# Moving the context projections of a five-stage decoder's fourth stage into its second stage, through DRAM

## The reference, cut to what matters

```
# second stage (first half): WKV over k = layernorm(x), v = ctx
y = wkv(w, u, k, v);  x = x + y
# fourth stage, per batch:
h  = layernorm(x)
q  = concat([ctx, h]) @ Wq                 # = ctx @ Wq[:256] + h @ Wq[256:]
k  = concat([h @ Wk,  ctx @ Wsk])          # 64 channels each
v  = concat([h @ Wv,  ctx @ Wsv])          # 64 channels each
x  = x + softmax(q k^T / sqrt(8) + alibi, windows 64 and 32) v @ Wo     # 32 query heads, 8 key heads
```

## Time and profile before

| | us |
|---|---|
| median of 3 runs | 808.35 |
| the runs | 806.6, 808.35, 809.21 |
| the profiled execution, as timed | 809.21 |
| its span, first to last instruction | 807.1 |

### The profile page before, as it was taken

One profiled execution on the slowest core, in us unless ns is written; L12 is line 12 of the kernel. 1 busy time (PEld: TensorE's weight loads), 2 busy tenths in 40 slices (PEclk: granted clock), 3 DMA queues, 4 the chain that ended last, 5 costly groups with the idle time before them and its releaser, 6 DMA issues.

```text
span 807.1 us, 19492 instructions
## 1 busy us (share of the span) xinstructions
PE 671.5 (83%) x6957; PEld 380.8 (47%) x6980; DVE 556.9 (69%) x1600; ACT 506.1 (63%) x1213; POOL 302.8 (38%) x488
## 2 busy tenths in 40 slices
PE   1789898854677589789999878999999999988985
PEld 0245555533445467444454444544455444544553
DVE  5478877688999994678787726455555555557776
ACT  3558888676677746388878743566555666565431
POOL 2214644295699958655565021112111211101110
PEclk9979999955689999899999999999999999999999
DMA  4757675200000001434535323322433234220001
GB/s 154 148 125 136 146 179 68 66 27 13 21 14 7 1 2 34 67 67 96 72 68 93 54 53 80 54 48 48 81 60 47 49 61 73 48 42 9 28 34 39
DMA packets 143104, 50.73 MB, mean 63 GB/s; under 512 B 131296, under 2 KB 140960, under 8 KB 142752
## 3 DMA queue, kind: packets, MB, share of 16 engines
q1 hardware_dynamic: 143008, 49.49, 31.1%
HBM read 15.64 MB, written 2.10 MB: 22 GB/s over the span
## 4 chain that ended last, share of the span: by engine, by line
PE 60%; DVE 13%; issue 9%; POOL 8%; ACT 6%; DMA 2%; SPq 1%; ACTq 0%; DVEq 0%; POOLq 0%
PE bank L1305 4%; PE bank L984 4%; PE bank L1255 3%; PE bank L946 3%; PE bank L1279 3%; PE bank L1237 2%; PE bank L959 2%; ACT l1x_probs L1199 2%; PE bank L995 2%; PE bank L1240 2%; PE bank L705 2%; PE bank L716 2%; PE bank L1331 2%; DVE l1a_neg_max L871 2%; PE bank L1005 2%
## 5 line engine op out<-in xcount | busy, mean ns | idle before, releaser
L1144 DVE TENSOR_REDUCE l1x_neg_max<-bank 128x2 f16<-128x448 f32 (+1 forms) x192 | 117.7, 636 | 98.9 <-PE bank L1262 98.9
L1199 ACT ACTIVATE l1x_probs<-bank 128x512 f32<-128x512 f32 x192 | 106.2, 596 | 41.9 <-PE bank L1283 24.9
L871 DVE TENSOR_REDUCE l1a_neg_max<-bank 128x4 f16<-128x512 f32 x128 | 83.3, 684 | 31.7 <-PE bank L959 31.0
L919 ACT ACTIVATE l1a_probs<-bank 128x512 f32<-128x512 f32 x128 | 69.7, 596 | 32.3 <-PE bank L973 31.2
L1097 POOL TENSOR_TENSOR l1x_rstd<-l1x_var_eps,minus_half 128x1 f32<-128x1 f32 x16 | 8.8, 548 | 203.4 <-DVE l1x_var_eps L1128 203.4
L1636 PE MATMUL bank<-mix_xT_parts,w_ternary 128*128 128x256 f16 x384 | 55.2, 302 | 14.4 <-DVE mix_hidden L1529 12.3
L558 DVE TENSOR_REDUCE l_neg_max<-bank 128x4 f16<-128x512 f32 x64 | 42.3, 684 | 17.4 <-PE bank L685 17.4
L1636 PEld LDWEIGHTS bank<-mix_xT_parts,w_ternary 128*128 128x128 f16 x384 | 39.5, 107 | 27.4 <-DVE mix_hidden L1529 11.4
L631 ACT ACTIVATE l_probs<-bank 128x512 f32<-128x512 f32 x64 | 36.8, 600 | 13.3 <-PE bank L705 13.3
L1460 POOL TENSOR_TENSOR mix_hidden_parts<-mix_hidden,mix_hidden_parts 128x256 f16<-128x256 f32 x48 | 35.8, 754 | 15.8 <-ACT mix_hidden_parts L1588 15.6
L1588 ACT CAST mix_hidden_parts<-mix_hidden 128x256 f16<-128x256 f32 x48 | 19.2, 403 | 31.2 <-DVE mix_hidden L1529 29.2
(11 more groups left out here) (268 smaller groups left out, 1877.3 us busy)
## 6 DMA issues: line engine op xcount, KB each, us to landing
x_residual<-x_in SPq DMA_DIRECT2D x4, 512.0 KB, 5.0
mix_ctx_in<-ctx_in SPq DMA_DIRECT2D x16, 128.0 KB, 2.0
l1x_ctx_in<-ctx_in SPq DMA_DIRECT2D x16, 128.0 KB, 2.1
out_dram<-moe_out SPq DMA_DIRECT2D x16, 128.0 KB, 1.7
w_f<-w_in SPq DMA_DIRECT2D x2, 704.0 KB, 6.3
w_attn_f<-w_l_in SPq DMA_DIRECT2D x1, 1024.0 KB, 6.8
q_stack<-q_begin_in SPq DMA_DIRECT2D x1, 1024.0 KB, 5.3
l1x_qT<-l1x_neg_maxT SPq DMA_DIRECT2D x64, 2.0 KB
```

The lines of the kernel that those rows point to most:

```text
L871: dve.tensor_reduce(mm[:, 16 * j + 4 * s:16 * j + 4 * s + 4], b_s[c % 3][:].rearrange("p (r k) -> p r k", k=P), AX.X, ALU.max, negate=True ...
L919: act.activation(prob[:, c, :], b_st[c % 2][:], ACT.Exp).then_inc(s_exp, 1)
L1144: dve.tensor_reduce(mm[:, first:first + count], scores, AX.X, ALU.max, negate=True).then_inc(s_max, 1)
L1199: act.activation(prob[:, c, :], b_st[c % 2][:], ACT.Exp).then_inc(s_exp, 1)
```

## The change

The second stage gets a piece `K` for each batch: PE multiplies the transposed context, which lies in SBUF as `vv`, by the 384 columns of `w_l1x_ctx`, into the batch's bank `b_kv[c]`; ACT copies the result to a buffer `cproj`; SP stores it to a new DRAM tensor `ctx_projected`. The bank is handed on only after that copy.

The fourth stage no longer loads or transposes the context. SP loads 320 of the 384 columns of a batch into `cp` (128 x 320), and brings the 64 V columns straight into the V tile `vs` with two DMAs of 64 rows each, in pieces of 8 numbers. `F7` is one projection of `x` with 384 columns. The high parts of the keys come from PSUM and from `cp`. The q of `x` and the q of the context are added by DVE (`F8`) into `pf`; ACT and POOL split `pf` into high and low parts. DVE makes the low part of the keys of `x` (`F8b`), POOL those of the context. V of `x` is copied by ACT in two instructions.

In the diff, the K pieces stand in the order SP, ACT, PE. The order tables of the second and the fourth stage are new on all engines, with their `PACE` entries, and those of the first and third stage keep their orders. PE's order in one turn of the fourth stage is now `ST.0 PV.1 S.3 ST.1 F5 S.4 T1.1 F7 ST.2 S.5 T4 ST.3 M T5 S.0 ST.4 PV.0 S.1 ST.5 T1.0 S.2`; SP's is `G X M V`. Two pairs of semaphores in the first stage are joined, scratch columns are kept apart, and two constants that place the FFN's weight preparation in the first stage move a little.

```diff
     ("mix", "sp"): order("""
-        W3.0+1 W3.1+1"""),
+        K.1-1 K.0 W3.0 W3.1"""),
     ("mix", "pe"): order("""
-        W3.1+1 HA.0-3 HA.1-3 G3-2 W11.0-1 HA.2-3 W3.0+2 W11.1-1 HA.3-3 HA.4-3 HA.5-3 D-4"""),
+        W3.1+1 K.0+1 W11.1-1 HA.3-3 G3-2 HA.4-3 HA.5-3 K.1+1 D-4 W3.0+2 HA.0-2 HA.1-2 HA.2-2 W11.0"""),
     ("l1x", "sp"): order("""
-        M-1 X+2 G+1"""),
+        G-2 X-1 M-3 V-3"""),
     ("l1x", "dve"): order("""
-        F1c+2 S.1 S.2 S.3 S.4 T1.0-2 F3+2 F1+3 S.5 S.6 T1b.0-2 T1.1-2 S.7 F1b+3 T1b.1-2 S.8 S.9 S.10 S.11 T5-2
-        S.0+1"""),
+        S.2 F1+3 S.3 S.4 F1b+3 T1.0-2 F3+2 S.5 S.6 T1b.0-2 S.7 S.8 T1.1-2 T1b.1-2 S.9 F8+2 S.10 S.11 F1c+3 T5-2
+        S.0+1 S.1+1 F8b+2"""),
     ("l1x", "act"): order("""
-        ST.0-1 V+1 ST.1-1 OE.1-2 F5+2 ST.2-1 ST.3-1 T4-2 ST.4-1 ST.5-1 F8a.0+2 F8a.1+2 ST.6-1 ST.7-1 M F8+2
-        OE.0-1 ST.8-1 ST.9-1 ST.10-1 ST.11-1"""),
+        ST.0-1 ST.1-1 V+1 OE.1-2 F5+2 ST.2-1 ST.3-1 F8a.0+2 ST.4-1 ST.5-1 T4-2 F8a.1+2 ST.6-1 M ST.7-1 ST.8-1
+        ST.9-1 OE.0-1 ST.10-1 ST.11-1"""),
     ("l1x", "pe"): order("""
-        PV.1-2 S.3 F5+2 ST.1-1 S.4 T1.1-2 F7+2 T4-2 ST.2-1 S.5 T5-2 ST.3-1 M S.0+1 PV.0-1 ST.4-1 S.1+1 ST.5-1
-        T1.0-1 S.2+1 ST.0"""),
+        ST.0-1 PV.1-2 S.3 ST.1-1 F5+2 S.4 T1.1-2 F7+2 ST.2-1 S.5 T4-2 ST.3-1 M T5-2 S.0+1 ST.4-1 PV.0-1 S.1+1
+        ST.5-1 T1.0-1 S.2+1"""),
-PACE = {"l0": (0, 8, 8.0, 11.73), "mix": (141.0, 2.25, 15.97, 7.96), "l1a": (270.0, 2.17, 8.18, 14.66), "l1x": (437.5, 5.91, 15.02, 26.37), "moe": (695.0, 5.96, 4.55, 4)}
+PACE = {"l0": (0, 8, 8.0, 11.73), "mix": (150.0, 1.35, 15.88, 5.97), "l1a": (263.0, 1.53, 8.18, 15.58), "l1x": (441.5, 6.93, 13.05, 26.37), "moe": (677.0, 5.96, 4.55, 4)}
...
+            if piece == "V":
+                wait(sp, s_pv, (b - 1) * 2)
+                for t in range(2):
+                    rows = slice(64 - 64 * t, 128 - 64 * t)
+                    sp.dma_start(vs[rows, b % 3, :, 32 * t:32 * t + D],
+                                 dram["ctx_projected"][b][64 * t:64 * t + 64, 320:384].rearrange("p (g d) -> p g d", d=D)).then_inc(s_vc[bp], 16)
...
+            elif piece == "F8":
+                dve.wait_ge(s_hi, 2 * b + 1)
+                wait(dve, s_lo, 2 * (b - 1))
+                dve.tensor_tensor(pf[:, bp, :], b_proj[:, 64:320], cp[:, bp, 0:C], ALU.add).then_inc(s_pf, 1)
+            elif piece == "F8b":
+                dve.wait_ge(s_pf, b + 1)
+                kf = b_proj[:, 0:64].rearrange("p (y d) -> p y d", d=D).unsqueeze(2).to_broadcast([P, 8, 2, D])
+                dve.tensor_tensor(k_slots[bp][:, 0:8, 1:4:2, :], kf, k_slots[bp][:, 0:8, 0:4:2, :], ALU.subtract).then_inc(s_lok, 1)
...
-                for t in range(2):
-                    for a in range(2):
-                        for e, w in enumerate((net.w_l1x_x, net.w_l1x_c)):
-                            pe.matmul(b_proj[64 * (e ^ t):64 * (e ^ t) + 64, 384 + 64 * t:448 + 64 * t], xt[:, 2 * e + a, 64 * t:64 * t + 64],
-                                      w[:, a, 320:384], start=a == 0, stop=a == 1, skip_group_check=True)
                 for a in range(2):
-                    pe.matmul(b_proj[:, 64:384], xt[:, 2 + a, :], net.w_l1x_c[:, a, 0:320], start=a == 0, stop=False,
-                              skip_group_check=True)
-                for a in range(2):
-                    ins = pe.matmul(b_proj[:, 0:320], xt[:, a, :], net.w_l1x_x[:, a, 0:320], start=False, stop=a == 1,
-                                    skip_group_check=True)
+                    ins = pe.matmul(b_proj[:, 0:384], xt[:, a, :], net.w_l1x_x[:, a, :], start=a == 0, stop=a == 1)
...
+            if piece == "K":
+                n = 2 * i + c
+                sp.wait_ge(s_cpo, n + 1)
+                sp.dma_start(dram["ctx_projected"][n], cproj[:]).then_inc(s_cps, 16)
...
+            elif piece == "K":
+                act.wait_ge(s_cp, n + 1)
+                wait(act, s_cps, 16 * n)
+                act.copy(cproj[:], b_kv[c][:, 0:384]).then_inc(s_cpo, 1)
...
-                wait(pe, s_kv, n - 1)
+                wait(pe, s_cpo, n - 1)
...
+            elif piece == "K":
+                if n == 0:
+                    pe.wait_ge(net.s_fit, FITTED)
+                pe.wait_ge(s_kv, n + 1)
+                for a in range(2):
+                    ins = pe.matmul(b_kv[c][:, 0:384], vv[:, c, a, :], net.w_l1x_c[:, a, :], start=a == 0, stop=a == 1)
+                ins.then_inc(s_cp, 1)
```

More of the change, by code:

```diff
@@ L564, in dve_program @@
                 dve.wait_ge(s_t3, b * 5 + 1)
-                wait(dve, s_to, b)
+                wait(dve, s_oq, 2 * b - 1)
                 dve.tensor_tensor(o[:].rearrange("p (y d) -> p y d", d=D), tail[:, :, 0:D],
@@ L637, in act_program @@
                 act.wait_ge(s_t3, b * 5 + 4)
-                wait(act, s_oq, b)
-                act.activation(to[:], o[:], ACT.Copy, bias=MAGIC, scale=omax[:, 2:3]).then_inc(s_to, 1)
+                wait(act, s_oq, 2 * b)
+                act.activation(to[:], o[:], ACT.Copy, bias=MAGIC, scale=omax[:, 2:3]).then_inc(s_oq, 1)
             elif piece == "T3e":
-                act.wait_ge(s_to, b + 1)
+                act.wait_ge(s_oq, 2 * b + 1)
                 wait(act, s_t4, b)
@@ L1063, in sp_program, with load_ctx @@
         sp.wait_ge(before.s_x, NB // 2)
-        sp.dma_start(ctx_in[:, 0, :], dram["ctx"][0]).then_inc(s_ctx[0], 16)
+        def load_ctx(b, bp):
+            src = dram["ctx_projected"][b]
+            sp.dma_start(cp[:, bp, :], src[:, 0:320]).then_inc(s_ctx[bp], 16)
+        sp.wait_ge(before.s_cps, 16 * NB)
+        load_ctx(0, 0)
         for at, piece, c, b, bp in pieces("l1x", "sp", NB):
@@ L1170, in act_program @@
                 wait(act, s_proj, b)
-                act.copy(xt[:].rearrange("p a t -> p (a t)"), b_proj[:]).then_inc(s_xt, 1)
-            elif piece == "F8":
-                act.wait_ge(s_proj, b + 1)
-                wait(act, s_lo, 3 * (b - 1))
-                act.copy(pf[:, bp, :], b_proj[:, 0:384]).then_inc(s_pf, 1)
+                act.copy(xt[:].rearrange("p a t -> p (a t)"), b_proj[:, 0:256]).then_inc(s_xt, 1)
             elif piece == "V":
-                act.wait_ge(s_proj, b + 1)
+                act.wait_ge(s_lok, b + 1)
@@ L1178, in act_program @@
                 wait(act, s_pv, (b - 2) * 2)
-                dst = vs[:, b % 3].rearrange("p g (t e) -> p t g e", t=2)[:, :, :, 0:D]
-                act.copy(dst, b_proj[:, 384:512].rearrange("p (t g d) -> p t g d", t=2, d=D)).then_inc(s_v, 1)
+                for t in range(2):
+                    rows = slice(64 * t, 64 * t + 64)
+                    ins = act.copy(vs[rows, b % 3, :, 32 * t:32 * t + D], b_proj[rows, 320:384].rearrange("p (g d) -> p g d", d=D))
+                ins.then_inc(s_v, 1)
@@ L1192, in act_program @@
+                    ins.then_inc(s_hi, 1)
+                else:
+                    act.wait_ge(s_pf, b + 1)
+                    src = pf[:, bp].rearrange("p (y d) -> p y d", d=D).unsqueeze(2).to_broadcast([P, 32, 2, D])
+                    act.copy(q_slots[bp][:, :, 0:2, :], src).then_inc(s_hi, 1)
             elif piece == "M":
@@ L1482, in norm_stats @@
             wait(dve, taken, 2 * pairs)
-            wait_apart(dve, sem, 3 * n + 1, net.dve_idle[:])
+            wait_apart(dve, sem, 3 * n + 1, net.dve_idle[:, 3:4])
             dve.bn_aggr(mv, stats[:]).then_inc(sem, 1)
```

111 lines of the change are left out of this document (50 added, 61 removed), and 10 rows, old and new, of the table TIMES.

## The result

| | before | after |
|---|---|---|
| median, us (4 runs each) | 807.59 | 773.51 |
| the runs, us | 806.6 to 809.21 | 773.14 to 775.38 |
| profiled execution, us | 809.21 | 773.48 |
| its span, us | 807.1 | 771.7 |
| busy us: PE, DVE, ACT, POOL | 671.5, 556.9, 506.1, 302.8 | 645.9, 572.1, 507.1, 297.1 |

The ratio of the times is 0.9574, with a 95% interval of 0.9546 to 0.9601: 34 us faster. The forecast was 781.0 with a range of 772 to 797.

The account below looks back on a forecast made before the run. PE's instruction time was taken to bound the fourth stage's turn, DVE the second stage. 809.21 - 24.3 (twelve turns) - 5 (other `F7`s) + 1.5 (`K`) = 781.4 us profiled, 781 against the median, range 772 to 797.

Parts of the forecast that it names:

- rival (b): Second stage: its new order gains by filling idle time of DVE and PE, 8 us less, 773 or below; chance 0.06.
- `F7` and the transposes, 1.88 us a turn: Fourth stage, PE: 2.97 us of `F7` and 0.22 of context transposes give way to one projection of 1.31 us.
- The waits, 0.15 us less: Fourth stage, PE waiting for ACT's `exp`: 0.65 to 0.95 us a turn where it was 0.94; turn 14.5 us.
- The other `F7`s, 5 us: Four `F7` executions outside the twelve turns: 5 of 7.5 us gained, between 0 and 8.
- DVE, ACT, the maxima: Fourth stage: DVE rises to 9.7 us a turn, ACT stays below 9.95, the maxima are no later; no cost.
- V, 1.4 us of SP: Fourth stage, SP's queue: two V loads of 512 pieces of 32 bytes take 1.4 us, ends 0 and 8.
- The limit 10.4 + V: Fourth stage, loop of maxima through SP: a turn cannot be under 10.4 us plus V's time, 11.8 at 1.4.
- `K` and the second stage, +1.5 us: Second stage: sixteen context projections mostly hidden beside DVE, the bound; +1.5 us, between -5 and +10.
- Rival (a): Waits on ACT grow in the fourth stage, or the second stage lengthens: 789 to 798 us; chance 0.24.
- (c): Fourth stage: V loads hold up the transposes, PE waits at `S.0`; 792 to 806 us, chance 0.03, or slower, 0.05.
- (d): Fourth stage: `F7` was not the price, PE's waits simply fill the time and nothing changes; chance 0.02.

## Why the prediction held, step by step

The time lies inside the range and the mechanism of the fourth stage came as told. It also lies 7.8 us below the sum, at the edge of what rival (b) was given (773 or below), and 5.6 of that came from a term that nobody had priced. That it is still inside owes something to the width of the range.

- **`F7` and the transposes, 1.88 us a turn: right.** PE's busy time of a turn fell by 15.59 - 13.71 = 1.88, and the kernel that changes only this shows that it comes off the turn in full (1.80 of 1.83).
- **The waits, 0.15 us less: mis-sized.** They fell from 0.94 to 0.49. The forecast expected some 0.5 ahead of `ST.3`, because the stretch from `ST.2` would hold 1.28 us of work, and 0.1 to 0.2 more for ACT's keys. The distance of 1.79 us was right to the hundredth (597.80 to 599.59), but PE's work in it is 1.48: `T4` counts 0.43 there and not 0.22. The keys were done when `ST.2` ended, and the 0.14 of PE's own issue is gone. Hence the turn of 14.20, below the 14.35 to 14.8 given. Over the eleven turns between the residual additions it is 25.3 us; the forecast counted twelve, from `F7` to `F7`, and at its 2.02 us each eleven are 22.2.
- **The other `F7`s, 5 us: too much.** The head gave 1.8, and the kernel without the context's work shows 7.5 there with before's order; the new order and starts gave 5.7 of it back. The end gave nothing: the three last turns and the fifth stage take the 95 us that they took. The first two of the last intervals between additions are 2.4 us shorter (12.80 and 14.36 for 14.54 and 15.00), the next two 2.3 longer (26.48 and 24.41 for 24.59 and 24.04).
- **DVE, ACT, the maxima: right.** DVE has 9.81 us a turn for the 9.7 given, and ACT 9.68. DVE, though, is nearer to the limit than "neither is near" says: the run with `T1.1` moved turned it into the one that PE waits for. The maxima were on time in this turn; once among the ten, at 577.83 us, PE waited 0.48 us for them, while a V pair took 2.17 us to issue.
- **V, 1.4 us of SP: right,** with 1.32, and the price of a short piece, 13 ns, is between the two that the forecast had. The limit 10.4 + V is right in size by some luck: the loop over the maxima is not what bound when V was four times as long, but the queue's sum, which is as long. By either, the change had about 2.4 us a turn to spare, and about 3.7 us for V would have begun to cost.
- **`K` and the second stage, +1.5 us: sign wrong, inside the bound.** `K` costs about 0.5 us. The way from the first stage's first addition to the third's is 2.9 us shorter with it; the new order of the second stage and the new starts are what is left to explain this, and which part does it was not tried. This is rival (b)'s mechanism with a third of its 8 us.
- **The two constants: no term at all.** The front names them; the prediction didn't price them, and they are worth 3 to 5 us by the medians; the first addition moved by 3.7 and 4.9 us in the two pairs, and by 5.6 between before and after. Counted by the forecast's terms: 24.3 + 5 - 1.5 = 27.8 us forecast, 25.3 + 1.8 + 2.9 = 30.0 measured, and 5.6 that had no term. These 2.2 and 5.6 are the distance from the sum of 781.4 to the profiled 773.5.

Rival (a) fell, as ACT lost more work than it gained; (c) came true at four times the V loads, with the wait at `S` and the time of before; (d) is excluded by the two kernels that change PE's work.

## What to carry to other kernels

When PE is busy for 94% of a turn and at full clock, price a change of its work by its busy time, one for one; price the order's waits by the distance between two dependent pieces less the work that is put between, each piece with its duration in that place. Orders of two engines that wait for each other move together: a move that is worth 0.7 us a turn in one kernel cost 1.0 in the other, where its counterparts were missing. Look at where stages join as well as at the turn: here the head gave back what the new order won in the turns. For a queue that only issues, sum its issues of one turn ahead of any loop through it. And read every line of a diff for what it starts earlier: three numbers that place three reductions of 1.74 us gave 3 to 5 of the 34 us.

## What the runs showed of the hardware that I had not expected

- A wait of 2.26 us on PE, with 0.22 us of work in 2 us, was followed by some 10 us at half clock, though PE was busy again for 1.5 to 2.0 of each 2 us; a wait of 0.60 at the same place was followed by none. Five profiled kernels show the one and nine the other.
- Work put into the gaps of a stage that has DVE busy for 87% raised PE's mean granted clock there, 0.73 to 0.86 from 155 to 250 us. The eight profiled kernels that have this work show 0.80 to 0.86.
- A pair of DMAs with 512 pieces of 32 bytes each takes 1.3 us of SP's queue, and now and then 2.0 to 2.2; on the 16 DMA engines it is about 13 ns for a packet, by the estimate above.
- SP's queue alone set a turn of 16.2 us when its issues summed to that, with PE waiting for its transposes in nine of ten turns.
